# A decoder layer with 64 experts on one NeuronCore: index lists, output buffers and shared-block adds of the expert stage

## The reference, cut to what matters

```python
logits = x @ gate_w.T                       # x: 4096 x 512, 64 experts
topk_w, topk_idx = top_k(softmax(logits), 6)
# each expert takes at most CAP = 128 of the tokens that chose it
g = silu(buf @ w_gate)                      # buf: 64 x 128 rows, F = 352
d = (g * (buf @ w_up)) @ w_down
y[t] = sum_k topk_w[t, k] * d[expert(t, k), place(t, k)]
y += (silu(x @ sh_gate.T) * (x @ sh_up.T)) @ sh_down.T
out = layernorm(x + y)
```

## Time and profile before

| what | value |
|---|---|
| median of 3 runs | 2021.44 us (2013.17 to 2021.53) |
| profiled execution, its own time | 2014.67 us |
| span of that execution | 2012.9 us |
| PE / DVE / ACT / POOL busy | 97% / 83% / 51% / 34% |
| expert adds (indirect, 128 rows) | 64 |
| shared adds (plain, 256 rows) | 12 |
| gathers | 64 |

### The profile page before, as it was taken

One profiled execution on the slowest core, in us unless ns is written; L12 is line 12 of the kernel. 1 busy time (PEld: TensorE's weight loads), 2 busy tenths in 40 slices (PEclk: granted clock), 3 DMA queues, 4 the chain that ended last, 5 costly groups with the idle time before them and its releaser, 6 DMA issues.

```text
span 2012.9 us, 42821 instructions
## 1 busy us (share of the span) xinstructions
PE 1953.1 (97%) x16720; PEld 1204.0 (60%) x16720; DVE 1667.5 (83%) x3829; ACT 1021.5 (51%) x1553; POOL 692.8 (34%) x710
## 2 busy tenths in 40 slices
PE   8999999999999999999999987899999999999998
PEld 3656666676666666667666653355555555555553
DVE  5557988988998999998999888658888888888767
ACT  5424535444453554445355354445665656566545
POOL 1002232232232222223222322434565455554623
PEclk9999999999999999999999989999999999999999
DMA  6810121122122022112201233589999999999948
GB/s 230 75 42 22 57 77 43 38 76 54 36 67 77 23 57 77 45 45 67 77 23 57 67 113 91 154 240 281 309 291 289 302 284 305 299 282 307 292 84 322
DMA packets 202021, 285.59 MB, mean 142 GB/s; under 512 B 100283, under 2 KB 110523, under 8 KB 201820
## 3 DMA queue, kind: packets, MB, share of 16 engines
q1 hardware_dynamic: 177692, 242.85, 38.7%
q0 software_dynamic: 24128, 40.01, 10.3%
HBM read 208.67 MB, written 57.42 MB: 132 GB/s over the span
## 4 chain that ended last, share of the span: by engine, by line
PE 83%; DVE 11%; ACT 2%; issue 2%; DMA 1%; POOL 1%; SPq 0%; ACTq 0%; POOLq 0%; DVEq 0%
PE ring L932 33%; PE moe_bank L1731 27%; PE ring L992 6%; DVE quad L1314 5%; PE moe_bank L1800 5%; PE fold L485 3%; PE ring L1056 2%; PE quad L1039 2%; PE moe_bank L1766 1%; DVE maxima L1314 1%; PE ring L1064 1%; PE moe_bank L1778 1%; DVE x_rows_split L1307 1%; DMA slot_table<-table_records,slot_of_choice 1%; PE fold L469 1%
## 5 line engine op out<-in xcount | busy, mean ns | idle before, releaser
L178 POOL DMA_INDIRECT slot_table<-table_records,slot_of_choice x204 | 203.8, 999 | 420.6 <-PE ring L932 316.8
L932 PE MATMUL ring<-tion_then_expert_weights,xT_split 128*128 128x512 f16 x1152 | 264.8, 379 | 1.9 <-DVE scratch L1266 1.9
L932 PE MATMUL ring<-xT_split,tion_then_expert_weights 128*128 128x256 f16 x2304 | 264.6, 273 | 0.0
L932 PEld LDWEIGHTS ring<-xT_split,tion_then_expert_weights 128*128 128x128 f16 x2304 | 222.9, 98 | 36.5 <-issue 2.4
L1168 ACT ACTIVATE scratch<-ring 128x512 f16<-128x512 f32 x192 | 114.0, 594 | 215.8 <-PE ring L932 215.8
L1680 POOL DMA_INDIRECT expert_sums<-tion_then_expert_weights,scatter_index x64 | 121.8, 1903 | 190.9 <-PE moe_bank L1731 58.9
L932 PEld LDWEIGHTS ring<-tion_then_expert_weights,xT_split 128*128 128x128 f16 x1152 | 109.0, 98 | 126.1 <-issue 4.7
L1314 DVE CUSTOM_DVE_ANT_0 quad<-quad,causal_penalty 128x128 f32<-128x128 f32 (+1 forms) x512 | 165.7, 396 | 11.0 <-PE quad L1022 9.7
L1266 DVE SCALAR_TENSOR_TENSOR scratch<-ring,scratch 128x512 f16<-128x512 f32 x192 | 128.9, 685 | 21.2 <-ACT scratch L1168 21.1
L932 PE MATMUL ring<-scratch,xT_split 128*128 128x256 f16 x1152 | 138.8, 273 | 0.0
L902 POOL TENSOR_SCALAR_AFFINE_SELECT scratch<-scratch 128x1024 f32<-128x1024 f32 x64 | 70.5, 1104 | 193.5 <-ACT scratch L1188 170.9
(11 more groups left out here) (248 smaller groups left out, 3962.5 us busy)
## 6 DMA issues: line engine op xcount, KB each, us to landing
gate_up_landing<-in_w_gate SPq DMA_DIRECT2D x43, 704.0 KB, 5.6
gate_up_landing<-in_w_up SPq DMA_DIRECT2D x43, 704.0 KB, 5.4
scratch<-in_w_down SPq DMA_DIRECT2D x43, 512.0 KB, 4.8
scratch<-in_w_gate SPq DMA_DIRECT2D x21, 704.0 KB, 5.5
scratch<-in_w_up SPq DMA_DIRECT2D x21, 704.0 KB, 5.9
tion_then_expert_weights<-in_w_down SPq DMA_DIRECT2D x21, 512.0 KB, 4.7
scratch<-in_w_down SPq DMA_DIRECT2D x43, 192.0 KB, 6.4
xT_in<-in_xT SPq DMA_DIRECT2D x16, 512.0 KB
```

What stands on the lines that cost most here:

```text
L178: pool.indirect_dma_start(self.dram, bass.IndirectOffsetOnAxis(ap=self.slot[:, tb, c:c + 1], axis=0), self.record[:, tb, c, :], None, boun ...
L932: last = pe.matmul(out_, left(a, c), right(b, c), start=(n == 0 and not onto), stop=(n == 3 * chunks - 1))
```

## The change

```diff
+OUTS = 3
...
-MOE_ADDS = places(s for s in MOE if s[0] == "D" or s[0] == "SD" and s[1] < LATE_DOWN and s[2] % 2)
+MOE_ADDS = places(s for s in MOE if s[0] == "D" or s[0] == "SD" and s[1] < LATE_DOWN)
...
-    gi = mem.sb("gather_index", [P, AHEAD, 1], U32)
-    si = mem.sb("scatter_index", [P, 2, 1], U32)
+    rows_of = mem.sb("rows_of_experts", [P, NX], U32)
+    rows_of_block = mem.sb("rows_of_blocks", [P, GROUP * LATE_DOWN], U32)
+    third = mem.sb("third_expert_out", [P, E], F32)
+    d32 = [loads.expert_out[:, 0, :], loads.expert_out[:, 1, :], third[:, :]]
...
-            index(gi[:, s, :], e)
...
         def add_expert(e):
...
-            if e >= 2:
-                pool.wait_ge(added, 16 * MOE_ADDS["D", e - 2])
             pool.wait_ge(free, MOE_FREED["D", e])
-            index(si[:, s, :], e)
...
         def add_shared(g, b):
...
-            pool.dma_start(moe_d[t * P:(t + 2) * P, :].rearrange("(t p) n -> p t n", p=P),
-                           sd32[:, b - 1:b + 1, :], accum_op=ALU.add).then_inc(added, 16)
+            pool.indirect_dma_start(moe_d, bass.IndirectOffsetOnAxis(ap=rows_of_block[:, k:k + 1], axis=0),
+                                    sd32[:, b, :], None, bounds_check=T + CAP - 1,
+                                    compute_op=ALU.add).then_inc(added, 16)
...
+        pool.iota(rows_of_block[:, :], pattern=[[P, GROUP * LATE_DOWN]], base=0, channel_multiplier=1,
+                  allow_small_or_imprecise_dtypes=True).then_inc(index_ready, 1)
+        pool.tensor_copy(rows_of[:, :], records[:, :, 0]).then_inc(index_ready, 1)
+        pool.wait_ge(index_ready, 2)
...
-                if e >= 2:
-                    dve.wait_ge(added, 16 * MOE_ADDS["D", e - 2])
-                dve.tensor_scalar(d32[:, e % 2, :], bank_of(step)[:, :], records[:, e:e + 1, 1].bitcast(F32),
+                if e >= OUTS:
+                    dve.wait_ge(added, 16 * MOE_ADDS["D", e - OUTS])
+                dve.tensor_scalar(d32[e % OUTS], bank_of(step)[:, :], records[:, e:e + 1, 1].bitcast(F32),
```

More of the change, by code:

```diff
@@ L1545, in experts @@
               WD=mem.sb("w_down_split", [P, 2, 2, FC * E], F16))
-    x2t, hs, ssilu32, sd32, d32 = loads.x2t, loads.hidden, loads.silu, loads.shared_out, loads.expert_out
+    x2t, hs, ssilu32, sd32 = loads.x2t, loads.hidden, loads.silu, loads.shared_out
     records = mem.sb("records", [P, NX, 2], U32)
-    gi = mem.sb("gather_index", [P, AHEAD, 1], U32)
-    si = mem.sb("scatter_index", [P, 2, 1], U32)
+    rows_of = mem.sb("rows_of_experts", [P, NX], U32)
+    rows_of_block = mem.sb("rows_of_blocks", [P, GROUP * LATE_DOWN], U32)
+    third = mem.sb("third_expert_out", [P, E], F32)
+    d32 = [loads.expert_out[:, 0, :], loads.expert_out[:, 1, :], third[:, :]]
     xg = mem.sb("gathered", [P, AHEAD, E], F32)
@@ L1647, in on_gpsimd @@
     def on_gpsimd(pool):
[L1648 to L1655, removed]
         def gather(e):
@@ L1662, in gather @@
                 pool.wait_ge(full, MOE_JOBS["X", e - AHEAD])
-            index(gi[:, s, :], e)
             own_wait(pool, taken)
             pool.indirect_dma_start(xg[:, s, :], None, x2_d,
-                                    bass.IndirectOffsetOnAxis(ap=gi[:, s, :], axis=0),
+                                    bass.IndirectOffsetOnAxis(ap=rows_of[:, e:e + 1], axis=0),
                                     bounds_check=T + CAP - 1).then_inc(gathered[s], 16)
         def add_expert(e):
-            s = e % 2
             n = MOE_ADDS["D", e]
-            if e >= 2:
-                pool.wait_ge(added, 16 * MOE_ADDS["D", e - 2])
             pool.wait_ge(free, MOE_FREED["D", e])
-            index(si[:, s, :], e)
             if n > 1:
@@ L1679, in add_expert @@
             own_wait(pool, taken)
-            pool.indirect_dma_start(moe_d, bass.IndirectOffsetOnAxis(ap=si[:, s, :], axis=0),
-                                    d32[:, s, :], None, bounds_check=T + CAP - 1,
+            pool.indirect_dma_start(moe_d, bass.IndirectOffsetOnAxis(ap=rows_of[:, e:e + 1], axis=0),
+                                    d32[e % OUTS], None, bounds_check=T + CAP - 1,
                                     compute_op=ALU.add).then_inc(added, 16)
         def add_shared(g, b):
-            n = MOE_ADDS["SD", g, b]
-            t = GROUP * g + b - 1
+            n, k = MOE_ADDS["SD", g, b], GROUP * g + b
             pool.wait_ge(free, MOE_FREED["SD", g, b])
@@ L1990, in on_vector @@
                 if e > 0:
-                    dve.wait_ge(added, 16 * MOE_ADDS["SD", e - 1, b | 1])
+                    dve.wait_ge(added, 16 * MOE_ADDS["SD", e - 1, b])
                 dve.tensor_scalar(sd32[:, b, :], bank_of(step)[:, :], 1.0 / W_SCALE, None, ALU.mult)\
```

## The result

The changed kernel took 2055.43 us in the median of 4 runs (2053.69 to 2061.2), beside 2018.24 us for the kernel before (4 runs, 2013.17 to 2021.53): a ratio of 1.0177, 95% interval 1.0135 to 1.0218. The profiled execution took 2054.1 us. It is slower, as forecast, and by more than the 16 us that the sum gave: the span grew by 39.2 us, from 2012.9 to 2052.1. The forecast was 2033 us, 22 us too low; the median lies 1.6 us inside the range of 2012 to 2057, and one of the four runs outside it. Four runs say little of the kernel before: 62 later ones, on three chips, took 2012 to 2049 us, with a median of 2024.5, and against that the ratio would be 1.015.

What follows compares the result with a forecast made beforehand. PE bounds the kernel, with the nearly full chain of adds as second resource. 60 - 25 - 16 - 3 = +16 us on 2014.67 gives 2030.7, plus a third of 6.8: 2033 us, range 2012 to 2057.

Steps and rivals of the forecast that it cites:

- Nothing that the change touches holds PE up today: Over the experts' stage: PE is busy 548.84 of 550 us, so the gain is capped at some 3 us.
- The chain is full: Adds each wait for the last to land; a period of 126.6 us in the stage was reckoned at 126.4, without idle time.
- Idle time was put at 25 us by medians: In the chain of adds over the whole stage of 604.4 us: about 25 us idle, 4%, set against the loss.
- Index copies at 0: On POOL: 128 copies go, one wider copy and one iota come; their removal changes the time by 0.
- The shared adds: In the chain: 10 pairs each become two adds landing in about 7.0 us, 60 us more in all.
- if the adds behind a shared one become ordinary: In the chain: adds following a shared one land in 7.0 us instead of 8.6, giving back up to 16 us.
- Slack at the end: Between the last add's landing, the row loads and DVE's final work: 3 us of lag absorbed.
- It doesn't matter where it shows: Chain lag up to 21 us goes to the row loads at the end; more stops DVE and then PE.
- The price of a third buffer at 0: DVE's wait for adds, 1.6 us, lies off PE's path; a third buffer allows 21 us of lag, two 11.
- The Trainium skill's fixed cost of 2.0 us: Per added DMA 2.0 + 0.85 us, ten of them 29 us, just the idle time, so nothing would be seen.
- The rival of the stall with loss of clock: Third rival, chance 0.04: stops also lower PE's clock in the last 300 us; 46 us plus some 10, 2070 us.
- The two sums for the worst case: Shared adds landing in 7.4 us: +40 us for the range's upper end, 46 us in the third rival.

Runs made afterwards that it cites:

- the lists alone: The kernel before with only the row lists added, plain adds of two blocks and two buffers kept: 2014.66 us, ratio 0.997.
- the split alone: The kernel before with only its 12 plain shared adds made 24 indirect adds of one block, copies and two buffers kept: 2095.62 us, ratio 1.0331.
- The one longer run with a profile: The longest run, 2032.59 us, of the kernel before with only the row lists added.

## Why the prediction was right, and where it was off

The direction and the mechanism held: a chain that was nearly full became overfull. The size did not: 16 us were forecast, 39 came, and the range held by 1.6 us at its upper end. Point by point:

- "Nothing that the change touches holds PE up today", a gain of 3 us at most: right for the profiled execution of 2014.67 us, since no shared adds at all give 2013 us with PE's busy time unchanged. It is wrong for most runs of the kernel before: their median is 2024.5, and three kernels with a lighter chain take 2013 to 2014. One profile, of one of the fastest runs, hid a gain of 10 us.
- The chain is full: right. Idle time was put at 25 us by medians; the gaps of the trace less 0.83 us for each handover are 32. In the changed kernel 3 are left.
- Index copies at 0: right within what can be told here (2063 against 2055 us with a wide spread). Whether they hold the chain back in some runs of the kernel before isn't shown: with the lists alone the ratio is 0.997, and its interval reaches 1.
- The shared adds: 60 us forecast, of which 8.5 are handovers; 58.0 in landings and 8.3 in handovers measured, 66. The nearest row, the expert's add, was the right one: 7.0 taken, 7.3 measured.
- The step that failed is what was set against the 60: 25 us of idle time and up to 16 "if the adds behind a shared one become ordinary", 41 together. They came to 23. Beside the kernel before, 29 us of idle time were used up, but the 16 did not come. The adds behind a shared one did become shorter (8.12 to 6.68 us on average up to 1900 us), yet those behind an expert's add grew from 6.77 to 7.37, and in sum the experts' landings grew by 6.1 us. Beside the kernel with lists and third buffer, from which the changed one differs in its shared adds alone, the experts' landings fall by 10.4 us (446.3 to 435.9) and 13 us of idle time are used up. Either way it is 23. How the two share it is open, for the sum of the experts' landings varies between kernels whose adds all fit (429.8 in the kernel before, 462.4 without any shared add). So 66 - 23 gives the 43 that are there; my 60 - 41 gave 19. The excess of a chain is a small difference of large terms.
- Slack at the end 3 us: 1.8 measured, plus 2.5 us that the chain started earlier.
- "It doesn't matter where it shows": right for the changed kernel. VectorE first stops for an add before its scale at 1562.62; the add that it waited for had been issued 25 us after its data was ready, where 21 were forecast. By the last expert VectorE's scale is 28.8 us late, and the other 12 us of the last add's 41 are lag, which goes to the row loads. The price of a third buffer at 0 was right only for the profiled run of the kernel before; in the full chain it is worth 33 us, because it keeps issues away from weight splits. The copy of this argument in my expectation for the split alone, "near 1995 us as in the changed kernel", missed by 43 us.
- The Trainium skill's fixed cost of 2.0 us (DMA: Bandwidth & Descriptors, Anatomy of one DMA), by which nothing would be seen: wrong here. The plain adds of one, two and four blocks have a fixed part of 4 to 5 us beside the weight loads.
- The rival of the stall with loss of clock was right in that PE lost clock, and wrong in that it costs time. The granted clock was 0.97 from 1500 to 1900 where it had been 1.00, and from 1300 us on the same matmuls keep PE busy for 711.07 us instead of 700.44. These 10.6 us and the 18 us for which PE stood idle between 1500 and 1900 add up to the 28.8 us above. But the adds hardly waited for PE's data: 3 us of idle time are left in the whole chain, so the slower matmuls lie beside it and can account for no more than that of the 43.5.
- The two sums for the worst case don't agree: 60 - 25 + 8 - 3 is 40, as under the range; the 46 of the third rival, from the same terms, doesn't come out.

## What to carry to other kernels

A series of transfers that each wait for the last is a resource of its own, and its load is the sum of landings and handovers, not the engine's busy time: reckon it for the fullest period before adding a link. Where it was full, larger and fewer transfers were the remedy here (12 plain adds in place of 24: 24 us), and their landing time must be read beside the traffic that runs there. Read it in more than one run, too: the profile of one of the fastest runs hid that the chain holds the kernel up in most of them. In this kernel pairs of blocks, row lists and three buffers, or one add for four blocks, take 2014 and 2013 us, 0.6 to 0.7% under the kernel before; both are at PE's floor of 2013.

## What was not expected of the hardware

- An adding DMA of 128, 256 or 512 contiguous rows of 2 KB landed in 6.3, 8.7 and 12.6 us in stages that move 284 to 294 GB/s in all; 128 contiguous rows by an index list took 7.3. Once the weights were in, an expert's add of 128 rows took only 4.9.
- The issue of an indirect DMA on GpSimd stretched from 1.6 to 3.13 us when a VectorE weight split of 1.6 to 1.75 us had begun just before it, and from 1.56 to 1.93 with an instruction of 0.53 us in the split's place; an issue that began before the split kept its length. Two engines released by one landing met in this way again and again.
- One program's runs spread from 2012 to 2038 us and a few beyond, and other forms of it by 2 to 3 us. The one longer run with a profile had more long issues and longer landings. Why a single run takes the one or the other is open.
- Why the indirect form lands 1.0 us later than the plain one is open too; its longer issue (1.7 against 0.95 us) is the nearest difference.
